# Head products in 44 columns instead of 48, and a second fold on GpSimd in a fused two-layer kernel

## What is computed

```python
x = x + tanh(g_xattn[0]) * L0_xattn(ctx, ctx, layernorm(x), ssm_kernel, D, 8)
x = x + tanh(g_ffn[0])   * L0_ffn(layernorm(x), ...)      # router over 64, top 8, LoRA
x = x + tanh(g_xattn[1]) * L1_xattn(layernorm(x), ctx, ...)  # 16 heads, int8 fake quantization
x = x + tanh(g_ffn[1])   * L1_ffn(layernorm(x), ...)      # 8 experts, top 2, and a shared one
```

```python
kv  = einsum('bhil,bhjl->bijhl', k_, v_)            # all products of two channels of a head
y   = causal convolution of kv along l with ssm_kernel[h]
out = einsum('bijhl,bhil->bjhl', y + kv * D, q_)    # sum over i with the query
```

## Time and profile before

| | |
|---|---|
| time, median of 3 runs | 197.13 us (197.11 to 197.26) |
| the profiled execution | 197.14 us |
| its span in the profile | 195.3 us |
| TensorE busy | 174.2 us, 89% |
| VectorE busy | 149.3 us, 76% |
| ScalarE busy | 113.3 us, 58% |
| GpSimd busy | 89.6 us, 46% |

### The profile page before, as it was taken

The page is one execution under the profiler, slowest core; times in us unless marked ns, Lnnn a source line. Parts: engine busy times, 40 slices in busy tenths (PEclk is TensorE's granted clock), DMA queues, the critical chain, the costliest instruction groups (busy, mean ns, idle before and its releaser), DMA issues.

```text
span 195.3 us, 3713 instructions
## 1 busy us (share of the span) xinstructions
PE 174.2 (89%) x1216; PEld 116.1 (59%) x1216; DVE 149.3 (76%) x432; ACT 113.3 (58%) x293; POOL 89.6 (46%) x137
## 2 busy tenths in 40 slices
PE   7989999998899999879768889879889989979991
PEld 8955555558466664635446665666568546735650
DVE  0888679864757789778999999998884898475754
ACT  2554044723342445562769999998799887344540
POOL 1169999997811222530193214152114589078000
PEclk9999999999999999999999999999999999999999
DMA  5989948000000000000000000000000085926983
GB/s 183 321 250 368 380 195 297 0 0 3 0 2 0 2 0 0 5 0 0 0 0 3 0 0 5 5 0 0 3 0 3 0 161 112 160 53 121 173 196 107
DMA packets 22770, 15.18 MB, mean 78 GB/s; under 512 B 17664, under 2 KB 21344, under 8 KB 22368
## 3 DMA queue, kind: packets, MB, share of 16 engines
q1 hardware_dynamic: 22112, 13.94, 26.5%
q10 hardware_dynamic: 640, 1.02, 1.4%
HBM read 9.68 MB, written 1.07 MB: 55 GB/s over the span
## 4 chain that ended last, share of the span: by engine, by line
PE 59%; ACT 16%; DVE 12%; issue 5%; DMA 4%; SPq 1%; DVEq 0%; ACTq 0%
PE PS L1721 7%; ACT R L714 5%; PE PS L1376 5%; PE PS L1468 5%; PE PS L1372 5%; PE PS L1373 5%; PE PS L1444 5%; DMA CT<-ctxr 4%; PE PS L1739 4%; ACT R L709 4%; PE PS L1399 3%; PE PS L1574 3%; PE PS L1411 3%; PE PS L1558 3%; PE PS L1544 2%
## 5 line engine op out<-in xcount | busy, mean ns | idle before, releaser
L476 POOL TENSOR_TENSOR R<-R,ROW 128x256 f32<-128x256 f32 x8 | 5.8, 735 | 32.1 <-ACT R L651 21.3
L1075 DVE TENSOR_REDUCE SM<-PS 128x8 f32<-128x1024 f32 x16 | 18.9, 1216 | 1.9 <-PE PS L1544 1.8
L1558 PE MATMUL PS<-CON,R 128*128 128x128 f32 x128 | 18.4, 276 | 1.4 <-ACT R L714 1.3
L521 POOL TENSOR_SCALAR R<-QT,SM 128x256 bf16<-128x256 f32 x32 | 15.8, 511 | 8.3 <-DVE SM L1154 8.0
L1311 DVE TENSOR_TENSOR R<-R,PS 128x512 bf16<-128x512 f32 (+1 forms) x17 | 11.6, 682 | 9.7 <-PE PS L1721 7.1
L349 POOL TENSOR_TENSOR R<-CT 128x512 f32<-128x512 f32 (+1 forms) x16 | 15.8, 985 | 6.6 <-DMA CT<-ctxr 6.6
L714 ACT ACTIVATE R<-PS 128x512 f32<-128x512 f32 x32 | 18.4, 606 | 0.2 <-PE PS L1558 0.2
L1721 PE MATMUL PS<-R 128*128 128x512 bf16 x64 | 16.4, 379 | 0.0
L846 ACT ACTIVATE R<-PS 128x512 f32<-128x512 f32 x17 | 10.1, 594 | 10.7 <-PE PS L1721 10.5
L1558 PEld LDWEIGHTS PS<-CON,R 128*128 128x128 f32 x128 | 14.3, 140 | 3.1 <-issue 2.7
L919 DVE TENSOR_TENSOR R<-PS,QT 128x512 f32<-128x512 f32 x16 | 11.0, 689 | 6.1 <-PE PS L1376 5.6
(11 more groups left out here) (158 smaller groups left out, 435.2 us busy)
## 6 DMA issues: line engine op xcount, KB each, us to landing
WST<-w SPq DMA_DIRECT2D x3, 1024.0 KB, 13.1
T_R<-lagged SPq DMA_DIRECT2D x2, 768.0 KB, 7.6
X<-x SPq DMA_DIRECT2D x2, 512.0 KB, 4.8
CT<-ctxr SPq DMA_DIRECT2D x2, 512.0 KB, 7.8
y<-X SPq DMA_DIRECT2D x8, 128.0 KB, 1.8
WQP<-wqp ACTq DMA_DIRECT2D x1, 512.0 KB, 6.9
WKV<-wkv SPq DMA_DIRECT2D x1, 512.0 KB, 11.5
R<-sw SPq DMA_DIRECT2D x3, 128.0 KB, 4.4
```

The costliest lines, as they stand in the source:

```text
L521: nc.gpsimd.tensor_scalar(XB[:, u % XS, j, :], MX[:, b, :], GG[:, b, e:e + 1], 1.0, ALU.mult, ALU.mult).then_inc(e_xb, 1)
L1075: V_.tensor_reduce(MX1[:, b % 2, 8 * c:8 * c + 8], S4[:, 8 * c:8 * c + 8, :], AX.X, ALU.max, negate=True).then_inc(a_mx, 1)
L1558: ins = TR(PS[:, 4 + k % 2, P * h:P * h + P], SS[:, b % 2, 4 * k + h, :], I)
```

## The change

The products of channels 4 to 7 with themselves are split once more. `upper` keeps its 32 columns; a new `middle` has channels 4 and 5 with channels 4 to 7, 8 columns; `lower` is left with channels 6 and 7 with themselves, 4 columns. KV has 44 columns a block (PAIRS), and a convolve matmul 352. `units_of` has five instructions (NPR) where it had three: the product with `upper`, its mirrored part, `middle`, its mirrored part, and `lower`, of 512, 256, 128, 64 and 64 elements a row. Everywhere that kv_d, kv_p or prod is counted, the counts follow.

`fold_again(b)` on GpSimd adds terms 2 and 3 of both halves of block b to terms 0 and 1, for blocks 3 to 7 (FOLD1), 512 elements a row. Blocks 3 and 4 are done right after the folds, 5 to 7 after bias_values(0) to (2). turn_sums waits for it (fold_more) and has 2 terms a half left, four instructions.

```diff
         fold = sem("fold")
+        fold_more = sem("fold_more")
         prod = sem("prod")
...
         PREP = 9
+        NPR = 5
+        PAIRS = 44
         FOLD0 = 2
         FOLD_H = 10
+        FOLD1 = 3
         WARM = 26
...
+        def middle(eng, h, lo=0, hi=AB):
+
+            k = CTH[:, lo:hi, HD0 * h + 4:HD0 * h + 8]
+            return eng.tensor_tensor(KV[:, h % RING, lo:hi, 32:40].rearrange("p c (i j) -> p c i j", i=2),
+                                     k[:, :, 0:2].unsqueeze(3).to_broadcast([P, hi - lo, 2, 4]),
+                                     k.unsqueeze(2).to_broadcast([P, hi - lo, 2, 4]), ALU.mult)
+
         def lower(eng, h, lo=0, hi=AB):
-            k = CTH[:, lo:hi, HD0 * h + 4:HD0 * h + 8]
-            return eng.tensor_tensor(KV[:, h % RING, lo:hi, 32:48].rearrange("p c (i j) -> p c i j", i=4),
-                                     k.unsqueeze(3).to_broadcast([P, hi - lo, 4, 4]),
-                                     k.unsqueeze(2).to_broadcast([P, hi - lo, 4, 4]), ALU.mult)
+            k = CTH[:, lo:hi, HD0 * h + 6:HD0 * h + 8]
+            return eng.tensor_tensor(KV[:, h % RING, lo:hi, 40:44].rearrange("p c (i j) -> p c i j", i=2),
+                                     k.unsqueeze(3).to_broadcast([P, hi - lo, 2, 2]),
+                                     k.unsqueeze(2).to_broadcast([P, hi - lo, 2, 2]), ALU.mult)
...
             upper(nc.gpsimd, 1, 0, NB).then_inc(kv_p, 1)
+            middle(nc.gpsimd, 1, 0, NB).then_inc(kv_p, 1)
             lower(nc.gpsimd, 1, 0, NB).then_inc(kv_p, 1)
...
             upper(nc.gpsimd, 1, NB, AB).then_inc(kv_p, 1)
+            middle(nc.gpsimd, 1, NB, AB).then_inc(kv_p, 1)
             lower(nc.gpsimd, 1, NB, AB).then_inc(kv_p, 1)
...
                 upper(nc.gpsimd, h).then_inc(kv_p, 1)
+                middle(nc.gpsimd, h).then_inc(kv_p, 1)
                 lower(nc.gpsimd, h).then_inc(kv_p, 1)
...
-                pool.wait_ge(prod, 3 * hi)
+                pool.wait_ge(prod, NPR * hi)
                 pair = PR[:, :, :, :, :].rearrange("p (a b) i h j -> p b a i (h j)", a=NL)[:, b]
...
                                         ).then_inc(fold, 1)
+
+            def fold_again(b):
+
+                pool.wait_ge(fold, NB - FOLD0 + b - FOLD0 + 1)
+                pair = PR[:, :, :, :, :].rearrange("p (a b) i h j -> p b a i (h j)", a=NL)[:, b]
+                nc.gpsimd.tensor_tensor(pair[:, :, 0:2], pair[:, :, 0:2], pair[:, :, 2:4], ALU.add
+                                        ).then_inc(fold_more, 1)
...
                     nc.gpsimd.memset(V[:, :, :, 17:VW], 0.0).then_inc(v_ones, 1)
+            fold_again(FOLD1)
+            fold_again(FOLD1 + 1)
             for b in range(NB - 3):
                 bias_values(b)
+                if b + FOLD1 + 2 < NB:
+                    fold_again(b + FOLD1 + 2)
                 if b == 2:
...
                 CU = C[:, :, 0:32].rearrange("p c (i j) -> p c i j", i=4)
-                q1 = q[:, :, 4:8].unsqueeze(3).to_broadcast([P, AB, 4, 4])
+                CM = C[:, :, 32:40].rearrange("p c (i j) -> p c i j", i=2)
+                q2 = q[:, :, 6:8].unsqueeze(3).to_broadcast([P, AB, 2, 2])
                 V_.tensor_tensor(PR[:, :, 0:4, h, :], CU, q[:, :, 0:4].unsqueeze(3).to_broadcast([P, AB, 4, 8]),
                                  ALU.mult).then_inc(prod, 1)
-                V_.tensor_tensor(PR[:, :, 4:8, h, 0:4], CU[:, :, :, 4:8].rearrange("p c j i -> p c i j"), q1, ALU.mult
+                V_.tensor_tensor(PR[:, :, 4:8, h, 0:4], CU[:, :, :, 4:8].rearrange("p c j i -> p c i j"),
+                                 q[:, :, 4:8].unsqueeze(3).to_broadcast([P, AB, 4, 4]), ALU.mult).then_inc(prod, 1)
+                V_.tensor_tensor(PR[:, :, 4:6, h, 4:8], CM, q[:, :, 4:6].unsqueeze(3).to_broadcast([P, AB, 2, 4]),
+                                 ALU.mult).then_inc(prod, 1)
+                V_.tensor_tensor(PR[:, :, 6:8, h, 4:6], CM[:, :, :, 2:4].rearrange("p c j i -> p c i j"), q2, ALU.mult
                                  ).then_inc(prod, 1)
-                V_.tensor_tensor(PR[:, :, 4:8, h, 4:8], C[:, :, 32:48].rearrange("p c (i j) -> p c i j", i=4), q1,
+                V_.tensor_tensor(PR[:, :, 6:8, h, 6:8], C[:, :, 40:44].rearrange("p c (i j) -> p c i j", i=2), q2,
                                  ALU.mult).then_inc(prod, 1)
...
             upper(V_, 0, 0, NB).then_inc(kv_d, 1)
+            middle(V_, 0, 0, NB).then_inc(kv_d, 1)
             lower(V_, 0, 0, NB).then_inc(kv_d, 1)
...
             upper(V_, 0, NB, AB).then_inc(kv_d, 1)
+            middle(V_, 0, NB, AB).then_inc(kv_d, 1)
             lower(V_, 0, NB, AB).then_inc(kv_d, 1)
...
                 if h == 0:
-                    pe.wait_ge(kv_d, 2)
+                    pe.wait_ge(kv_d, 3)
                 else:
-                    pe.wait_ge(kv_p, 2 * h + 2)
+                    pe.wait_ge(kv_p, 3 * h + 3)
                 if h == 2:
...
                 if h >= 3:
-                    pe.wait_ge(prod, 3 * (h - 2))
-                kv = KV[:, h % RING, :, 0:48]
+                    pe.wait_ge(prod, NPR * (h - 2))
+                kv = KV[:, h % RING, :, 0:PAIRS]
                 at = 2 * (h % 3)
-                one, two = (PS[:, k, :].rearrange("p (b c) -> p b c", b=NB)[:, :, 0:48] for k in (at, at + 1))
+                one, two = (PS[:, k, :].rearrange("p (b c) -> p b c", b=NB)[:, :, 0:PAIRS] for k in (at, at + 1))
                 M(one, T[:, h, 0:P], kv[:, 0:NB], start=True, stop=True)
...
                 if h == 0:
-                    pe.wait_ge(kv_d, 4)
+                    pe.wait_ge(kv_d, 6)
                 M(two, T[:, h, 0:P], kv[:, NB:2 * NB], start=False, stop=True).then_inc(conv, 1)
...
                     else:
-                        pe.wait_ge(prod, 3 * NH0)
+                        pe.wait_ge(prod, NPR * NH0)
                 ins = M(PS[:, 4, :], WKV[:, k, P * c:P * c + P],
...
                 if b == 0:
-                    pe.wait_ge(prod, 3 * NH0)
+                    pe.wait_ge(prod, NPR * NH0)
                 if b >= 2:
...
                     terms = 4
+                if b >= FOLD1:
+                    pe.wait_ge(fold_more, b - FOLD1 + 1)
+                    terms = 2
                 for a in range(NL):
```

## The result

| | before | after |
|---|---|---|
| time, median of 4 runs | 197.19 us (197.11 to 197.29) | 195.26 us (195.04 to 195.48) |
| ratio, 95% interval | | 0.9905 (0.989 to 0.9919) |
| the profiled execution, its span | 197.14, 195.3 us | 195.42, 193.6 us |

The kernel is faster by 1.93 us; 3.2 were forecast. The time lies 1.36 us above the forecast, and 0.46 us above the top of its range. Two stages did nearly what they were to do, and a third, which the forecast took as moving along unchanged, gave 0.9 us back.

What follows compares the result with a forecast made beforehand. TensorE was taken to bound the kernel, with 59% of the chain. Sum: 197.14 - 2.47 (columns) + 0.11 (VectorE's last head) - 1.74 (fewer terms) + 0.9 (VectorE stalled by GpSimd) = 193.94, forecast 193.9 us, range 192.8 to 194.8.

Steps and rivals of the forecast that it cites:

- Two stages: Head convolutions: 2.47 us saved, 0.11 lost on VectorE's last head; feed-forward: 1.74 saved by shorter turn_sums, 0.9 lost to a stall.
- a third: Everything behind the feed-forward stage, with the last DMA transposes: the forecast's sum had no term for it, and no rival covered it.

## What to carry to other kernels

A sum over the stages that a change touches is not finished before the last wait of the kernel has been asked whether it has slack: look for the transfers that the end hangs on, and see in the DMA view what else passes there, instruction packets too. When a second engine gets more work beside VectorE, list VectorE's instructions that will come due in that stretch one by one: moving the single fold that collided (with block 6's left out) gave about 1 us, spreading all of them gave nothing. If half of a change beats the whole, the halves are disturbing each other, and the chain shows where.

## What the runs showed of the hardware

- One 16 KB instruction packet among DMA transposes brought the DMA down from some 160 to 215 GB/s to 5 to 17 for a microsecond, and a transpose from 3.2 to 4.7 to 5.0 us. It cost 0.8 to 1.0 us when the last two transposes were hit, nothing when earlier ones were.
- 128 instructions that only wait on a satisfied semaphore took TensorE 13.75 us at its end, 107 ns each, and made the kernel 10.0 us longer; where it had matmuls queued they cost nothing that shows.
- VectorE's f_rows, 0.41 us alone, took 1.66 us beside a GpSimd memset, and 3.00 us when three of GpSimd's instructions followed each other directly; but once it came in between two folds and took 0.41.
